# Decoder layer kernel on one core: the block that holds all five engine programs is opened without the GpSimd drain at its end

## The chip, the cores and the metric

The kernel runs on one core of one Trainium2 chip. The metric is device time in microseconds (us) of one launch. The kernel before was timed three times: 584.96, 585.82 and 586.62 us, median 585.82 us. It is written in Bass: every engine has a program of its own, and engines wait for one another by semaphores that the code names.

## The reference

One pre-norm decoder layer in float32, on x of shape (2, 1024, 256), so 2048 tokens of width 256. Cut to what is computed:

```
x = x + linear_attention(layernorm(x))      # phi(q), phi(k), k*v; two decayed prefix scans over 1024 steps
x = x + cross_attention(layernorm(x), ctx)  # 16 heads, 154 context rows, weights fside, a mask, softmax
h = layernorm(x)
y = sum over the 2 experts of 8 that each token picks: w * expert(h)    # 256 -> 352 -> 256, silu
z = shared_expert(h)
return x + y + z
```

## The kernel before, in words

`decoder(nc, A, xs, out)` (L172) allocates all buffers and semaphores, and at L378 opens one block with `nc.Block()`. In it stand five functions: the programs of TensorE (L380), ScalarE (L818), VectorE (L1071), GpSimd (L1639) and SyncE (L1791). There is no scheduler: each engine runs its program in the order in which it is written. Tokens are worked on in 16 tiles of 128, or in 4 chunks of 512. When the functions have ended, leaving the block joins the engines: this adds to each engine's program a few closing instructions, and the profile files them under L173, the line of the `with` statement whose end closes the block.

The last stage is that of the routed experts. Rows of tokens were sorted by expert into `xs_dram`; 36 slots of 128 such rows go through their expert. For each slot GpSimd issues an indirect DMA that adds the slot's 128 result rows of 256 floats to the token rows of `out_dram` (`add`, L1761; the four mixed slots take two such DMAs of 64 rows, so there are 40). Another 32 indirect DMAs of GpSimd scatter rows into `xs_dram` (L1685) earlier on. These 72 are all the DMAs that GpSimd issues; the descriptors of such a DMA are made by GpSimd itself, so each shows as a busy instruction there. All transfers that SyncE and ScalarE issue go through other queues.

Each add DMA counts up one of two semaphores, `to_out[0]` and `to_out[1]`, in turn, and a later add mostly waits for the one before it, since two slots may touch the same token. The end of the kernel is the last of these adds. SyncE's program ends with waits, so that nothing leaves the block before all of `out_dram` is written:

```
            w.wait_ge(base_out, 64)
            w.wait_ge(base_out3, 16)
            for a in (LAST[-1] - 1, LAST[-1]):
                w.wait_ge(to_out[a % 2], added(a))
```

GpSimd's own program has nothing behind its last add: it branches to the end of the block.

The closing instructions of the block use two semaphores, which stand in the program as `barrier_Pool_Activation_PE_DVE_SP_gather` and `..._release` (Pool is GpSimd, Activation ScalarE). The four other engines each raise gather by one. GpSimd waits until gather is 4, takes the 4 off again, and raises release by 4; each of the four waits for release and takes one off. The same exchange, drain of GpSimd and all, stands once at the start of the program (filed under L1997).

Of the kernel before, what the change touches and what calls it, by code (L numbers as in the profile page):

```python
# [171 lines left out]
def decoder(nc, A, xs, out):  # L172
    with ExitStack() as ctx:  # L173
# [201 lines left out]
            k, c = kc  # L375
            return bank[("pj", c, "q", 1) if k == 1 else ("q", 2 * c + 1, 7) if k == 2 else ("sm", c, 1, 2)]

        block = ctx.enter_context(nc.Block())  # L378

        @block.tensor  # L380
        def _(e):
# [1625 lines left out]
```

## Time and profile before

| what | us |
|---|---|
| median of three runs | 585.82 |
| lowest, highest | 584.96, 586.62 |
| span of the profiled execution, first to last instruction | 582.9 |
| PE (TensorE matmul) busy | 562.7 (97%) |
| DVE (VectorE) busy | 441.9 (76%) |
| ACT (ScalarE) busy | 326.0 (56%) |
| POOL (GpSimd) busy | 233.1 (40%) |

The profile is of one execution. It gives that execution's time as its span, from the first to the last instruction of the program; a device time of its own is not recorded for it. What lies around the span is what the launch adds ahead of the first and behind the last instruction, and the profile shows no instructions there; median less span is 585.82 - 582.9 = 2.9 us.

How to read the views: an engine's name with a q behind it (POOLq, SPq) is that engine's sequencer, the part that takes instructions in order, waits on semaphores and issues DMAs. Sequencer instructions are not counted as busy, so a drain never shows in the busy shares. The view of one line lists its instructions by engine and operation: how many, their durations in ns (least, median, most), and when the first and last of them began in us. EVENT_SEMAPHORE is an instruction that only waits on or changes a semaphore. DRAIN is a sequencer instruction too; its duration is the time that it stood there. DMA_INDIRECT as a busy instruction of POOL is the making of the descriptors; the transfer comes during and after it.

### The profile page before, as it was taken

What the parts mean: (1) busy time and instruction counts of PE and PEld (TensorE: products, weight loads), DVE (VectorE), ACT (ScalarE), POOL (GpSimd) and SP (SyncE); (2) the same over time, 40 slices, a digit from 0 to 9 for tenths busy, and PEclk for the clock granted to TensorE, in tenths of its full rate; (3) what the DMA queues carried; (4) which work ended last, traced back from release to release, by engine and by line L of the source; (5) the groups of instructions that cost most, each with busy time, mean ns of one, the idle gap of its engine ahead of it and who ended that gap; (6) DMA issues with size and microseconds to landing.
All of it is one profiled execution on the core that took longest, in us unless ns stands there. A gap on an engine that the chain in (4) does not pass through costs nothing.

```text
span 582.9 us, 11123 instructions
## 1 busy us (share of the span) xinstructions
PE 562.7 (97%) x3656; PEld 426.1 (73%) x3656; DVE 441.9 (76%) x838; ACT 326.0 (56%) x1005; POOL 233.1 (40%) x228
## 2 busy tenths in 40 slices
PE   8999999999999999999999999999999999999991
PEld 6547566788697978888788787878777776666661
DVE  3999999999886879958688679866677555656650
ACT  3632424368869796795976939715223245455220
POOL 1110110307580834387234671625235333353443
PEclk9999999999999999999999999999999999999997
DMA  8930004162741231423316107892645443344323
GB/s 301 347 101 2 1 1 172 45 217 91 274 155 65 100 119 45 173 74 93 127 37 218 65 20 230 270 390 87 181 111 90 67 64 58 53 70 61 54 29 35
DMA packets 36183, 68.37 MB, mean 117 GB/s; under 512 B 5504, under 2 KB 29024, under 8 KB 33632
## 3 DMA queue, kind: packets, MB, share of 16 engines
q1 hardware_dynamic: 28208, 57.99, 29.7%
q0 software_dynamic: 6784, 8.95, 9.5%
q10 hardware_dynamic: 1136, 0.73, 0.4%
q8 instruction: 30, 0.49, 0.4%
q14 instruction: 25, 0.20, 0.1%
HBM read 56.62 MB, written 15.25 MB: 123 GB/s over the span
## 4 chain that ended last, share of the span: by engine, by line
PE 58%; DVE 18%; DMA 9%; issue 7%; POOL 3%; ACT 2%; POOLq 1%; SPq 0%; DVEq 0%
PE pb L744 9%; PE pb L636 6%; DVE R L1140 6%; PE pb L499 6%; PE pb L601 6%; PE pb L549 6%; DMA out_dram<-R 5%; PE pb L565 5%; PE pb L778 5%; PE pb L516 4%; PE pb L648 3%; DVE R L1163 3%; DMA x<-in_x_dram 2%; DMA out_dram<-R,hidx 2%; PE pb L569 2%
## 5 line engine op out<-in xcount | busy, mean ns | idle before, releaser
L896 ACT ACTIVATE R<-R,mx 128x154 f32<-128x154 f32 x256 | 104.4, 415 | 0.2
L1761 POOL DMA_INDIRECT out_dram<-R x36 | 55.8, 1549 | 80.3 <-DMA out_dram<-R 33.9
L744 PE MATMUL pb<-R 128*128 x256 | 81.0, 459 | 0.0
L1022 ACT ACTIVATE R<-R 128x352 f32<-128x352 f32 x36 | 17.9, 497 | 91.6 <-DVE R L1572 80.3
L744 PEld LDWEIGHTS pb<-R 128*128 128x128 f32 x256 | 46.2, 190 | 20.4
L499 PE MATMUL pb<-xnT,wq 128*128 128x256 f32 x256 | 58.2, 383 | 0.0
L887 ACT ACTIVATE R<-pb,bq 128x256 f32<-128x256 f32 x64 | 30.1, 474 | 47.9 <-PE pb L499 47.8
L499 PEld LDWEIGHTS pb<-xnT,wq 128*128 128x128 f32 x256 | 47.7, 190 | 7.8 <-issue 1.2
L908 ACT COPY R<-pb 128x512 f32<-128x512 f32 x80 | 40.8, 614 | 18.4 <-PE pb L549 18.3
L1685 POOL DMA_INDIRECT xs_dram<-xn,pos x32 | 31.8, 993 | 47.3 <-DVE pos L1324 39.0
L896 ACT ACTIVATION_READ_ACCUMULATOR R<-R,mx 128x1 f32 x256 | 49.5, 193 | 0.0
L1660 POOL TENSOR_TENSOR sd<-mv,cst 128x4 f32<-128x4 f32 x12 | 9.8, 813 | 97.4 <-DVE mv L1088 97.3
L1219 DVE SCALAR_TENSOR_TENSOR R<-R 128x2464 f32<-128x2464 uint8 (+1 forms) x18 | 48.7, 2711 | 0.0
L778 PE MATMUL pb<-R 128*128 (+1 forms) x192 | 47.1, 381 | 1.5 <-ACT R L1031 1.5
L1208 DVE TENSOR_TENSOR R<-pb,R 128x924 f32<-128x924 f32 (+1 forms) x48 | 45.2, 998 | 2.7 <-PE pb L516 2.0
L1226 DVE TENSOR_REDUCE mx<-R 128x16 f32<-128x2464 f32 (+1 forms) x18 | 43.7, 2429 | 0.3
L636 PE MATMUL pb<-xnT,sw 128*128 128x256 f32 (+1 forms) x192 | 43.4, 381 | 0.0
L440 PE MATMUL pb<-xnT,R 128*128 128x512 f32 x96 | 43.0, 599 | 0.3 <-ACT xnT L831 0.3
L601 PE MATMUL pb<-wo,R 128*128 128x256 f32 x192 | 42.5, 380 | 0.0
L601 PEld LDWEIGHTS pb<-wo,R 128*128 128x128 f32 x192 | 36.4, 190 | 5.4 <-issue 0.4
L636 PEld LDWEIGHTS pb<-xnT,sw 128*128 128x128 f32 (+1 forms) x192 | 34.2, 181 | 7.1 <-issue 0.8
L778 PEld LDWEIGHTS pb<-R 128*128 128x128 f32 (+1 forms) x192 | 34.0, 191 | 5.7 <-issue 2.4
(202 smaller groups left out, 1180.1 us busy)
## 6 DMA issues: line engine op xcount, KB each, us to landing
R<-in_fside_dram SPq DMA_DIRECT2D x16, 1232.0 KB, 5.5
R<-in_L_ffn_w_dram SPq DMA_DIRECT2D x16, 352.0 KB
R<-in_mask_dram SPq DMA_DIRECT2D x16, 308.0 KB, 2.9
R<-xs_dram SPq DMA_DIRECT2D x32, 129.0 KB, 2.1
KV<-in_ebias_dram SPq DMA_DIRECT2D x2, 1440.0 KB
out_dram<-x SPq DMA_DIRECT2D x4, 512.0 KB, 4.7
R<-in_L_ffn_w_dram SPq DMA_DIRECT2D x8, 256.0 KB, 4.5
x<-in_x_dram SPq DMA_DIRECT2D x3, 512.0 KB, 11.4
```

Source lines behind the costliest of these rows:

```text
L440: ins = e.matmul(pb[:, u.i, :], wqkv[:, k, col * P:(col + 1) * P], xnT[:, r, k, :], start=(k == 0), stop=(k == 1))
L499: ins = e.matmul(pb[:, u.i, 0:256], wq[:, k, j * P:(j + 1) * P], xnT[:, r, k, cols], start=(k == 0), stop=(k == 1))
L601: ins = e.matmul(pb[:, u.i, 0:D], oT[:, j, q * P:(q + 1) * P], wo[:, j, :], start=(j == 0), stop=(j == 7))
L636: ins = e.matmul(pb[0:mw, u.i, q * 256:q * 256 + 256], wm[:, k, lo:lo + mw], xnT[:, r, k, cols], start=(k == 0), stop=(k == 1))
L744: ins = e.matmul(pb[:, u.i, 0:F], xsT[:, s % 2, k, :], ew13[:, bass.ds(w_reg[s] * 1408 + q * 704 + k * F, F)], start=(k == 0), stop=(k == 1))
L778: ins = e.matmul(pb[:, u.i, 0:D], sT[0:mw, s % 2, m, :], ew2[0:mw, bass.ds(w_reg[s] * 768 + m * D, D)], start=(m == 0), stop=(m == 2))
L896: ins = e.activation(att[t % 3][:, h, :], att[t % 3][:, h, :], ACT.Exp, bias=mx[:, a4, 1, h:h + 1], accum_out=mx[:, a4, 2, h:h + 1])
L908: e.copy(pT[:, hf, 2 * k:2 * k + 2, :], pb[:, u.i, :].rearrange("p (i q) -> p i q", i=2)).then_inc(free[u.i], 1)
L1208: e.tensor_tensor(att[t % 3][:, 2 * lo:2 * hi, :].rearrange("p (r h) k -> p r h k", r=2), pb[:, u.i:u.i + 2, 0:n * SK].rearrange("p r (h k ...
L1219: e.scalar_tensor_tensor(out=att[t % 3][:, lo:hi, :], in0=mk[:, s, lo:hi, :], scalar=-BIG, in1=att[t % 3][:, lo:hi, :], op0=ALU.mult, op1= ...
L1226: e.tensor_reduce(mx[:, a4, 0, lo:hi], att[t % 3][:, lo:hi, :], AX.X, ALU.max).then_inc(*topped.next((t, hs, 0)))
L1761: e.indirect_dma_start(out=out, out_offset=bass.IndirectOffsetOnAxis(ap=to.bitcast(U32), axis=0), in_=rows, in_offset=None, compute_op=ALU ...
```

## The change

One argument where the block is opened:

```diff
@@ -375,7 +375,7 @@
-        block = ctx.enter_context(nc.Block())
+        block = ctx.enter_context(nc.Block(no_gpsimd_drain=True))
 
         @block.tensor
         def _(e):
```

The five engine programs are untouched: 1105 rows of TensorE, 932 of VectorE, 406 of ScalarE, 234 of GpSimd and 286 of SyncE stand as they did, in the same order. Only the closing instructions of the block differ. In the built program they are:

```
before
  ScalarE, TensorE, VectorE, SyncE, each:
    Drain            waits release == 0, then gather + 1
    EventSemaphore   waits release >= 1, then release - 1
  GpSimd:
    Drain            (no semaphore)
    EventSemaphore   waits gather >= 4, then gather - 4
    EventSemaphore   release + 4
after
  ScalarE, TensorE, VectorE, SyncE, each:
    Drain            (no semaphore)
    EventSemaphore   waits release == 0, then gather + 1
    EventSemaphore   waits release >= 1, then release - 1
  GpSimd:
    EventSemaphore   waits gather >= 4, then gather - 4
    EventSemaphore   release + 4
```

So GpSimd's Drain is gone, and the other four have their drain and their count on gather in two instructions, where it was one. That makes 5 drains and 6 semaphore instructions before, and 4 drains and 10 semaphore instructions after. The exchange at the start of the program, with its drain, is not changed.

## Rows read from the trace of the kernel before

**Rows 1.** The page: span, busy time by engine, and the chain by engine and line.

```profile
span 582.9 us, 11123 instructions
PE 562.7 (97%) x3656; PEld 426.1 (73%) x3656; DVE 441.9 (76%) x838; ACT 326.0 (56%) x1005; POOL 233.1 (40%) x228
PE 58%; DVE 18%; DMA 9%; issue 7%; POOL 3%; ACT 2%; POOLq 1%; SPq 0%; DVEq 0%
```

**Rows 2.** The chain that ended last, its end: start us, us, what.

```profile
570.59 3.42 DMA out_dram<-R
574.01 0.88 issue
574.89 1.78 POOLq L173
```

**Rows 3.** View of line L173, the block's end.

```profile
L173 POOLq EVENT_SEMAPHORE  x2: 17/17/17, 582.7 to 582.7; - x2
L173 ACTq DRAIN  x1: 521/521/521, 569.2 to 569.2; - x1
L173 PEldq DRAIN  x1: 1320/1320/1320, 570.1 to 570.1; - x1
L173 DVEq DRAIN  x1: 524/524/524, 571.4 to 571.4; - x1
L173 POOLq DRAIN  x1: 7731/7731/7731, 574.9 to 574.9; - x1
L173 SPq COMPARE_BRANCH  x1: 41/41/41, 579.0 to 579.0; - x1
L173 SPq DRAIN  x1: 7/7/7, 579.2 to 579.2; - x1
L173 SPq EVENT_SEMAPHORE  x1: 17/17/17, 582.8 to 582.8; - x1
L173 PEldq EVENT_SEMAPHORE  x1: 51/51/51, 582.8 to 582.8; - x1
```

**Rows 4.** Timeline from 574 us: start us, us, engine, what [idle before].

```profile
572.45 1.56 POOL L1761 DMA_INDIRECT out_dram<-R  x1 [0.30 <-issue]
575.11 1.55 POOL L1761 DMA_INDIRECT out_dram<-R  x1 [1.10 <-issue]
```

**Rows 5.** Sequencer waits of SyncE from 568 us: total, times, longest.

```profile
SPq L86 <- DMA out_dram<-R: 28.0, 2, 25.3
SPq L173 <- PEq L173: 3.6, 1, 3.6
```

**Rows 6.** View of line L86, the wait helper, from 574 us.

```profile
L86 SPq EVENT_SEMAPHORE  x2: 17/22/28, 576.2 to 579.0; - x2
```

**Rows 7.** Stretches of the tail: busy by engine, PEclk, DMA share, GB/s.

```profile
576.00:578.00 2.00, 0.00 (x0) 0.00 (x0) 0.00 (x0) 0.00 (x0) 0.66 (x1) 0.50 0.40 28
578.00:580.00 2.00, 0.00 (x0) 0.00 (x0) 0.00 (x0) 0.00 (x0) 0.00 (x0) 0.50 0.25 38
580.00:582.90 2.90, 0.00 (x0) 0.00 (x0) 0.00 (x0) 0.00 (x0) 0.00 (x0) 0.50 0.00 0
```

**Rows 8.** View of line L1997, the exchange at the program's start.

```profile
L1997 DVEq DRAIN  x1: 10/10/10, 0.1 to 0.1; - x1
L1997 POOLq DRAIN  x1: 169/169/169, 0.3 to 0.3; - x1
L1997 PEldq EVENT_SEMAPHORE  x1: 51/51/51, 0.7 to 0.7; - x1
```

**Rows 9.** DMA view, issues by GpSimd: line, engine, operation, count.

```profile
out_dram<-R POOLq DMA_INDIRECT x36
xs_dram<-xn,pos POOLq DMA_INDIRECT x32
out_dram<-R,hidx POOLq DMA_INDIRECT x4
```

## The prediction

> **What bounds the kernel now.** I read the page first, then the end of the chain of waits, then the one line that the change touches, and last the stretches of the tail. The page [rows 1] says that TensorE is busy for 562.7 of 582.9 us and that the chain is 58% PE. A change that touches no matmul can still move the time, though, if it touches the part in which TensorE is no longer the bound. The chain [rows 2] shows where that is: from 570.59 us on it holds a transfer of the last adds (3.42), a wait that no record explains (0.88), and then GpSimd's sequencer in line L173 (1.78). It ends at 574.89 + 1.78 = 576.67. That is not the end of the span: the chain is followed back from the last *busy* instruction, and the last busy instruction is GpSimd's making of the descriptors of the final add, from 575.11 for 1.55 us, so to 576.66 [rows 4]. What lies behind it, 582.9 - 576.7 = 6.2 us, is in no chain and in no busy share. The reader should notice this: the chain gives GpSimd's sequencer 1% of the span, and the change acts on just the part that it leaves out.
>
> The view of the line that closes the block fills the gap [rows 3]. GpSimd's DRAIN begins at 574.9 and stands for 7731 ns, so to 574.89 + 7.73 = 582.62. Its two semaphore instructions follow at 582.7, and the other engines' last ones at 582.8; TensorE's ends at 582.8 + 0.051, and that is the end of the span. All others had been at the end of the block long before: ScalarE at 569.2, TensorE at 570.1, VectorE at 571.4, SyncE at 579.2. SyncE is the last of them since it waits for the data: its two waits on the adds ran off at 576.2 and 579.0 [rows 6], the second being the landing of the very last add. From then on it stood 3.6 us in the closing exchange [rows 5] (the row puts it down to PEq, which had been done for nine microseconds; by the rule that a wait is given to the last poster seen, the true one is GpSimd's release). The stretches agree [rows 7]: in 576 to 578 and 578 to 580 us the DMA engines are still at 0.40 and 0.25; in 580 to 582.9 they are at 0.00, and so is everything else. For 2.9 us and more the chip does nothing that the kernel needs: the drain alone holds the end.
>
> **The change part by part.**
>
> GpSimd's DRAIN goes. Before, the end is set by the later of two arrivals, the drain's end at 582.62 and SyncE's count at 579.2. Without the drain GpSimd is at its wait on gather from 574.9 on, and what is late next is SyncE, and thus the landing of the last add. That landing does not move by this edit, as the add is issued before the block's end on the same engine in both kernels.
>
> The exchange itself stays. From the end of the drain to the end of the span it took 582.85 - 582.62 = 0.23 us. The same exchange at the start of the program [rows 8] gives a second price: from the drain's end at 0.3 + 0.17 = 0.5 to TensorE's end at 0.7 + 0.05 = 0.75 it took some 0.25 us (rounded rows, so 0.2 to 0.3). I take 0.23.
>
> Four drains and four counts become separate instructions. Three engines have 7 us and more to spare. On SyncE the count now comes one instruction later than its DRAIN of 7 ns: a semaphore instruction of SyncE costs 17 to 28 ns [rows 3, 6], and the nearest gap between two of its instructions is that from the branch (579.0 + 0.04) to the drain (579.2), some 0.1 to 0.2. So between 0.02 and 0.2 us; I take 0.05, near to the instruction's own duration, since no branch lies between. It can't be below nothing: an instruction is added in front of the count.
>
> The sum: SyncE's drain at 579.2, plus 0.05 for its own count, plus 0.23 for the exchange, gives an end at 579.5 us. Span before 582.9, so the change takes away 582.9 - 579.5 = 3.4 us (bounds 3.2 with the slow end of both terms, 3.5 with the fast end). The launch's surroundings of 2.9 us I leave as they are. The profiled execution with its 582.9 + 2.9 stands for the median here, as the 2.9 is the median less the span. So 585.8 - 3.4 = **582.4 us**, 0.58% less. About 0.3%, or 1.8 us, is what a measurement of this kernel can tell from no change (its three runs lie within 1.66 us), so a gain of 3.4 is visible.
>
> What the drain waits for is the one open quantity, and it matters for the rivals. It outlasts the landing of the last transfer at 579.0 by 582.62 - 579.0 = 3.6 us, so it is not just a wait for the data. The drain at the start of the program, with no DMA of GpSimd behind it, took 169 ns [rows 8]. At the end 36 + 32 + 4 = 72 of them lie behind it [rows 9]. From the end of the last descriptor-making, 576.66, to the drain's end are 5.96 us, which would be 0.083 us for each of the 72. Either reading (3.6 us after the landing, or 5.96 of work from 576.66 on) fits this one trace; both drop out of the span when the DRAIN does.
>
> **Rivals.**
>
> *The drain is only put off.* Behind the program the launch has an ending of its own, part of the 2.9 us around the span. If that ending needs GpSimd to be idle in the same sense, then what was paid in the block is paid there: GpSimd would be ready at 582.62 as before, whoever asks. The span in the profile would shrink by 3.4 and the time would not, 585.8 us. For it: 2.9 us is room for instructions on all engines, and the program's own start has such a drain. Against it: the trace shows none behind the span, and data has landed at 579.0, so nothing needs waiting for. The start's drain of 169 ns [rows 8] and the 3.6 us left over here weigh about alike, and I give it one chance in five.
>
> The Trainium skill bears on this: "VectorE: DVE Perf Modes", section "The DRAIN you can't avoid", tells of drains that the runtime adds ahead of and behind a program on all five engines, about 12 ns each. No row here shows those behind the span. If there is one on GpSimd, it stands at 12 ns only because the block's drain came before it, and without that it would be the one that takes the 3.6 us; by this rule the time stays at 585.8. "Runtime: NRT & Kernel Launch", section "The ~15µs preamble/postamble breakdown", adds that resetting semaphores and re-arming DMA rings ends every launch; by that the ending has a reset of its own, which need not wait. By that second page the time would follow the span.
>
> *The drain is put off and starts over; slower.* This is the second reading of the open quantity: the 5.96 us are work of GpSimd that starts when it is asked for (0.083 us for each of the 72 DMAs). Before, 579.2 - 576.66 = 2.5 us of it lay beside the last transfer. If the launch's ending asks for it, it starts only at 579.5, runs alone, and ends at 579.5 + 5.96 = 585.5, where it was 582.62 (plus the exchange, 582.85): 2.6 us later, 588.4 us. It decides against me if both hold, that the ending asks and that the work is by the count of DMAs. For it: 3.6 us after the last landing is hard to explain by waiting. Against: what was against the first rival.
>
> *It doesn't do what it says.* The argument acts on the closing instructions alone; the drain at the start is left (169 ns, hidden behind nothing, no change). GpSimd's drain is gone in the built program, so I give this no chance of its own. A variant is that the last add's landing comes later or earlier by chance: adds take 3.4 us of transfer each in the chain [rows 2], and a few tenths of scatter go into the range.
>
> **How the numbers follow.** Forecast, 3.4 us less at 582.4: 0.72. Put off at equal price, 585.8: 0.19. Put off and started over, 588.4: 0.07. The rest, 0.02, is a gain that comes out under 0.3%, split between the ending and the span. The likeliest case has its own range: the sum's bounds are 582.3 to 582.6, and the scatter of medians (runs 0.9 below and 0.8 above theirs) widens it to 581.5 to 583.3. That holds nearly all of its 0.72. To leave out no more than 2 in 10 it has to reach into the first rival, to 586.0, which takes in a half of it and more. Range 581.4 to 586.0. Chances: faster by over 0.3% (below 584.1) 0.72; within 0.3% 0.20; slower by over 0.3% (above 587.6) 0.08.
>
> **What the profile of the changed kernel would show.** The view of L173 has no POOLq DRAIN; it has two semaphore instructions each on ACTq, PEldq, DVEq and SPq, and two on POOLq, the first of which begins within 0.1 us of SyncE's count. SyncE's wait in the closing exchange falls from 3.6 to about 0.2 us. The span is 579.5 us, give or take 0.3, and the stretch behind the last landing is 0.5 us long. Everything up to 575 us stands at the same times within 0.2. If the span is 579.5 and the time stays near 585.8, the drain was put off; if the time is near 588.4, it was put off and starts over. The forecast is wrong altogether if the span itself stays near 582.9, for then something else than the drain held GpSimd.

## The result: 0.54% faster, by the drain that left the end

| | median us | lowest, highest | runs |
|---|---|---|---|
| kernel before | 586.14 | 584.96, 587.65 | 6 |
| changed kernel | 582.54 | 581.2, 583.38 | 6 |

The ratio is 0.9946, 95% interval 0.9932 to 0.996: 3.2 us less, 2.3 to 4.0 (the two medians of the table lie 3.6 us apart, within that interval). Timed again beside other kernels (five runs of it, 15 of before) it was 0.9956, 0.9943 to 0.997, so 2.6 us, 1.8 to 3.3. The forecast was 582.4 us, 3.4 us less.

For the six runs of the changed kernel, and for all runs of the experiments below, the span of each run is recorded too. Kept apart: the kernel before has a median span of 583.95 us (28 runs, beside e1 to e4) and 583.3 (15 runs, beside e5 to e8), the changed one of 580.6 (6 runs) and 580.7 (5). What lies around the span, the time less the span, was 1.81 to 1.82 us in the median for the kernel before, and 1.92 to 1.94 for the changed one.

### The profile page after: what moved, and what is told of

Its sections match the earlier page's. It is cut to its first block, busy times and chain, and to the rows that moved or that the text cites. A ratio compares the mean times of both kernels' runs of the same rounds, so it can differ in the third digit from the quotient of the medians.

```text
span 581.5 us, 11126 instructions
## 1 busy us (share of the span) xinstructions
PE 562.7 (97%) x3656; PEld 426.0 (73%) x3656; DVE 441.7 (76%) x838; ACT 326.0 (56%) x1005; POOL 232.7 (40%) x228
## 4 chain that ended last, share of the span: by engine, by line
PE 56%; DVE 20%; DMA 9%; issue 8%; POOL 4%; ACT 2%; POOLq 0%; DVEq 0%; SPq 0%
PE pb L744 7%; DMA out_dram<-R 6%; PE pb L636 6%; DVE R L1140 6%; PE pb L499 6%; PE pb L601 6%; PE pb L549 6%; PE pb L565 5%; PE pb L516 4%; PE pb L648 4%; PE pb L778 4%; DVE R L1163 3%; PE pb L613 2%; PE pb L569 2%; DMA out_dram<-R,hidx 2%
```

## The profile after

The profiled execution of the changed kernel took 583.38 us with a span of 581.5. The busy times on the page are those of before but for tenths, as in [rows 1]; there are three instructions more, 11126.

```profile
span 581.5 us, 11126 instructions
PE 562.7 (97%) x3656; PEld 426.0 (73%) x3656; DVE 441.7 (76%) x838; ACT 326.0 (56%) x1005; POOL 232.7 (40%) x228
```

The view of L173, which answers to [rows 3]; the columns are count, durations in ns, and when the first and last began:

```profile
L173 PEldq EVENT_SEMAPHORE  x2: 51/51/51, 571.4 to 581.4; - x2
L173 SPq EVENT_SEMAPHORE  x2: 17/17/17, 581.2 to 581.4; - x2
L173 POOLq EVENT_SEMAPHORE  x2: 17/17/17, 581.3 to 581.3; - x2
...
L173 SPq COMPARE_BRANCH  x1: 41/41/41, 581.0 to 581.0; - x1
L173 SPq DRAIN  x1: 7/7/7, 581.2 to 581.2; - x1
```

There is no POOLq DRAIN. SyncE's drain begins at 581.2, its count on gather follows at 581.2, GpSimd answers at 581.3, and TensorE's last semaphore instruction ends at 581.45. SyncE's waits, as in [rows 5]:

```profile
SPq L86 <- DMA out_dram<-R: 28.5, 2, 25.7
SPq L173 <- PEq L173: 0.2, 1, 0.2
```

Where SyncE stood 3.6 us in the closing exchange, it stands 0.2. The order of the ends has turned round: the landing of the last add, which ends SyncE's second wait at 580.9, now sets the end.

```profile
L86 SPq EVENT_SEMAPHORE  x2: 17/22/28, 578.1 to 580.9; - x2
```

The end of the chain, against [rows 2]:

```profile
572.50 3.42 DMA out_dram<-R
575.92 1.11 issue
577.03 1.55 POOL out_dram L1761
```

The GpSimd sequencer in L173 is gone from it. The chain again stops at the last descriptor-making (577.03 + 1.55 = 578.58), so the landing and the exchange, 2.9 us, stand in it no more than the drain did. But the reader should see another thing: the last descriptor-making begins at 577.03, where it was 575.11 in [rows 4]. The whole tail stands 1.9 us later than in the profile of before. The span of this pair of profiles therefore fell by 1.4 us only, while the times fell by 3.2. The experiments say which of the two to believe.

## The experiments

Three readings of the drain were open: it ends a fixed time after the last landing; it is work of a fixed price from the moment at which GpSimd is free; or it is work by the count of DMAs. And one rival on the time: that it is only put off. "Engine free" below is the end of the last descriptor-making, 576.66 us in the profile of before.

**The drain put back by hand.** `e1_own_drain` is the changed kernel with this at the end of GpSimd's program:

```diff
                 if s < 4:
                     scatter_rows(3, 1, s)
+            e.drain()
```

> The block is opened without the GpSimd drain, as in the changed kernel, and GpSimd's own program ends with one explicit drain. If the drain alone was what cost 3.6 us, it comes back whole: a POOLq DRAIN of about 7.7 us, ending 3.7 us after the last landing, and the time of the kernel before (ratio 1.00). If the gain came from the other form of the closing exchange (counts in instructions of their own), the time stays near that of the changed kernel (0.994).

Measured: ratio to before 1.0009, 0.9991 to 1.0027. The explicit drain:

```profile
L1790 POOLq DRAIN  x1: 7731/7731/7731, 576.0 to 576.0; - x1
```

7731 ns, the same to the nanosecond as in [rows 3], though this execution reached it 1.2 us later. So the instruction alone is the cost, not the form of the exchange. One small thing does go with the form: the time less the span is 1.92 us here as in the changed kernel, against 1.82 in those that keep the old closing exchange. The changed form gives back 0.1 us outside the span; why is open.

**The drain asked for after the landing.** `e2_land_then_drain`, on the kernel before:

```diff
                 if s < 4:
                     scatter_rows(3, 1, s)
+            for a in (LAST[-1] - 1, LAST[-1]):
+                w.wait_ge(to_out[a % 2], added(a))
```

> The kernel before, but GpSimd waits for the last two adds to land ahead of the block's drain. Theory landing (the drain ends a fixed 3.6 us after the last landing, whenever it was asked for): DRAIN lasts 3.6 us, time as before (ratio 1.00). Theory work (5.96 us of work from the moment it is asked for with GpSimd free): DRAIN lasts 6.0 us from the landing, the span ends 2.3 us later, ratio 1.004. Theory plain wait (the drain only waits for data): DRAIN under 0.3 us, ratio 0.994.

Measured: ratio 1.0056, 1.004 to 1.0071.

```profile
L173 POOLq DRAIN  x1: 5948/5948/5948, 579.0 to 579.0; - x1
```

All data had landed, and the drain still took 5.95 us, as it does from the engine's being free in the kernel before (574.89 + 7.73 - 576.66 = 5.96). The reading "fixed time after the landing" falls: the drain is work that starts when asked for. This also prices the overlap that the kernel before had, some 2.3 us beside the last transfer (the span of this execution is 2.3 us longer; the times say 3.3 us, 2.3 to 4.2).

**A second drain early, and two in a row.** `e3_mid_drain` and `e4_two_drains`, both on the kernel before. The first added drain is that of e3 alone, the second that of e4 alone:

```diff
             add_sb2(3)
+            e.drain()                      # e3
             w.wait_ge(placed.sem, placed[3])
...
                     scatter_rows(3, 1, s)
+            e.drain()                      # e4
```

> The kernel before with one more drain in GpSimd's program, behind 24 of its 72 DMAs, where it waits for VectorE anyway (ahead of the scatter of the last chunk). Theory count (0.083 us for each GpSimd DMA not yet drained): the middle drain lasts 24 x 0.083 = 2.0 us though all its data landed long ago, and the last one has 48 DMAs to do: it ends at 576.66 + 4.0 = 580.6 us where it was 582.6, ratio 0.997. Theory landing: the middle drain lasts 0.2 us or less, the last one ends 3.6 us after the landing as before, ratio 1.00. Theory work with a fixed price: the middle drain lasts 6.0 us, the last one as before, ratio 1.00.

> The kernel before with an explicit drain of GpSimd straight ahead of the block's own, so two in a row at the end. Theories count and landing: the first takes 7.7 us as the single one did, the second finds nothing to do and lasts 0.2 us or less, ratio 1.00. Theory fixed price: the second costs 3.6 to 6.0 us more, ratio 1.006 to 1.010.

Measured: e3 0.9969 (0.9948 to 0.9991), e4 1.0002 (0.9983 to 1.0021). In e3 the early drain stood for 9663 ns from 397.3, most of it behind work that GpSimd had queued; its last instruction ahead of the drain ended at 404.87, so 2.05 us were its own. The last drain of e3, and the two of e4:

```profile
L173 POOLq DRAIN  x1: 6056/6056/6056, 575.0 to 575.0; - x1
```

```profile
L1790 POOLq DRAIN  x1: 7731/7731/7731, 576.7 to 576.7; - x1
...
L173 POOLq DRAIN  x1: 47/47/47, 584.5 to 584.5; - x1
```

24 DMAs, 2.05 us; 48 DMAs, 575.0 + 6.06 less the engine's being free at 576.77, 4.28 us (count says 4.0; the 0.3 us over it are not explained); 72 DMAs, 5.96; none, 0.05. So the price is by the DMAs that GpSimd has issued since its last drain, long landed or not. The fixed price falls with e4. A drain put where GpSimd waits anyway takes its share off the end: e3 is 1.8 us faster than before (0.5 to 3.0) by doing more.

**More DMAs.** Three kernels issue 48 more DMAs in the idle stretches of GpSimd before 100 us, each 8 bytes of 16 rows (`e5_48_small`) or of 128 rows (`e6_48_large`; `e7_48_large_no_drain` is the same on the changed kernel), and `e11_40_large` 40 of 128 rows. The edit, in e6:

```diff
+        spare = sb("spare", (P, 48, 2))
+        extra = sem("extra")
...
-            for kc in NORMS[0:6]:
+            for n, kc in enumerate(NORMS[0:6]):
                 rooting(*kc)
+                if n in (2, 3, 4):
+                    for i in range(16):
+                        e.dma_start(spare[0:128, 16 * (n - 2) + i, :], A["cst"][0:128, 0:2]).then_inc(extra, 16)
+            e.wait_ge(extra, 16 * 48)
             add_bo(0)
```

> The kernel before with 48 more DMAs issued by GpSimd between 35 and 100 us, where it is idle; each moves 16 rows of 8 bytes into a spare tile that nobody reads. Theory count of DMAs (0.07 to 0.083 us each, whatever their size): the last drain ends 3.4 to 4.0 us later against the end of the last descriptor-making (9.4 to 9.9 us behind it where it was 5.95), ratio 1.006 to 1.007. Theory count of rows (the cost goes by the descriptors, 128 or 64 rows for each of the 72): 48 x 16 rows are 8% more than 72 x 128, the drain takes 0.4 to 0.5 us more, ratio 1.001. A rival, that only indirect DMAs cost: nothing is added, ratio 1.00.

> As the run with 48 more small DMAs, but each of the 48 moves 128 rows of 8 bytes. Theory count of DMAs: the same drain as with 16 rows, 9.4 to 9.9 us behind the last descriptor-making. Theory count of rows: 48 x 128 rows are 67% more, so again 9.4 to 9.9 us, but only 6.4 us with 16 rows. Ratio 1.006 to 1.007 for both theories; the pair of runs tells them apart.

> The changed kernel (no GpSimd drain at the block's end) with the same 48 more DMAs of 128 rows. If the drain is only put off into the launch's ending, the time less the span grows from 1.9 us by what 120 DMAs cost there (3 us and more). If it is gone, the time less the span stays 1.9 us and the time is that of the changed kernel, ratio 0.994 to 0.995 against the kernel before, though the same kernel with the drain is at 1.006.

Measured: e5 1.0068 (1.0053 to 1.0084), e6 1.0014 (1.0001 to 1.0027), e7 0.9947 (0.9932 to 0.9962). The last drains of e5 and, below it, e6:

```profile
L173 POOLq DRAIN  x1: 11652/11652/11652, 577.6 to 577.6; - x1
```

```profile
L173 POOLq DRAIN  x1: 7733/7733/7733, 576.1 to 576.1; - x1
```

e5 is as the count has it: 3.92 us more for 48, 0.0817 us each. e6 is what neither theory allowed: 48 larger DMAs added 2 ns. The chain of e6 shows one trace of the 48. Between the wait that ends with a landing and the making of the third last add's descriptors, GpSimd stands 0.61 us longer than in the kernel before; here that piece, first before, then in e6:

```profile
569.88 0.49 issue
```

```profile
570.55 1.10 issue
```

This pause comes after 117 of the 120 DMAs, and e7 has it at the same place. It is about what e6 is slower by (0.8 us, 0.1 to 1.6).

e7 does its own task all the same. With 120 DMAs issued, of which a drain would have counted 72 by e6, and no drain, the time less the span is 1.90 us and the time that of the changed kernel, so nothing of the drain is paid in the launch's ending. That ends both rivals in which it is put off. Nor does the exchange at the start of a program show it: GpSimd's drain there is as short in the changed kernel as in [rows 8], and as in e1, which drains at its end.

```profile
L1997 POOLq DRAIN  x1: 171/171/171, 0.3 to 0.3; - x1
```

**What a drain costs, measured by itself.** To see why e6 paid nothing, two kernels on the changed one put groups of such DMAs early, wait for them to land, and drain. Each ran once, and only its drains are read. The edit in `e9_drain_ladder`, with `spare` and `extra` as in e6:

```diff
-            for kc in NORMS[0:6]:
+            issued = 0
+            groups = {0: ((4, 16),), 1: ((16, 16),), 2: ((16, 128),), 3: ((32, 128),), 4: ((16, 64),)}
+            for n, kc in enumerate(NORMS[0:6]):
                 rooting(*kc)
+                for many, few in groups.get(n, ()):
+                    for i in range(many):
+                        e.dma_start(spare[0:few, i, :], A["cst"][0:few, 0:2]).then_inc(extra, 16)
+                    issued += many
+                if n in groups:
+                    e.wait_ge(extra, 16 * issued)
+                    e.drain()
```

> The changed kernel, with five groups of extra DMAs in the stretches before 110 us where GpSimd is idle, each group waited for until it has landed and then followed by an explicit drain: 4 of 16 rows, 16 of 16 rows, 16 of 128 rows, 32 of 128 rows, 16 of 64 rows. As all data has landed, each drain shows the bookkeeping alone. Theory count, with old entries given up when room is needed (so that the run with 48 DMAs of 128 rows had lost them by the end): drains of 0.3, 1.3, 1.3, 2.6 and 1.3 us, by 0.082 us each, whatever the rows. Theory size (a DMA of 128 rows of 8 bytes leaves no entry, one of 16 does): 0.3, 1.3, under 0.2, under 0.2 and, for 64 rows, one or the other. The time of the whole says nothing, since the groups delay GpSimd.

The five drains of e9, each from the view of its line in a stretch of its own:

```profile
L1729 POOLq DRAIN  x1: 387/387/387, 15.6 to 15.6; - x1
...
L1729 POOLq DRAIN  x1: 1344/1344/1344, 33.9 to 33.9; - x1
...
L1729 POOLq DRAIN  x1: 1350/1350/1350, 47.6 to 47.6; - x1
...
L1729 POOLq DRAIN  x1: 2651/2651/2651, 82.2 to 82.2; - x1
...
L1729 POOLq DRAIN  x1: 1344/1344/1344, 98.3 to 98.3; - x1
```

4, 16, 16, 32 and 16 DMAs: 0.06 us and (2651 - 387) / 28 = 81 ns for each, whether of 16, 64 or 128 rows. The count holds, and the size does not matter to the drain. `e10_long_ladder` has the groups 48, 72, 96 and 120 of 128 rows and 120 of 16, with a wait for landing after each 48:

> The changed kernel with five groups of extra DMAs early in GpSimd's program, each waited for and then drained: 48, 72, 96 and 120 of 128 rows, and 120 of 16 rows. With nothing given up the drains take 0.06 + 0.0816 us for each: 4.0, 5.9, 7.9, 9.9 and 9.9 us. If old entries are given up once their rows fill the room there is, the drains of the large ones stop growing with a group somewhere between 72 and 120 (the run with 48 large ones ahead of the 72 of the kernel showed only 72), or fall back, while 120 of 16 rows still take 9.9 us. The time of the whole says nothing, as the groups delay GpSimd by hundreds of us in all.

```profile
L1731 POOLq DRAIN  x1: 3986/3986/3986, 44.2 to 44.2; - x1
...
L1731 POOLq DRAIN  x1: 5922/5922/5922, 92.0 to 92.0; - x1
...
L1731 POOLq DRAIN  x1: 7877/7877/7877, 158.4 to 158.4; - x1
...
L1731 POOLq DRAIN  x1: 609/609/609, 241.8 to 241.8; - x1
...
L1731 POOLq DRAIN  x1: 9837/9837/9837, 306.3 to 306.3; - x1
```

72 are 5.92 us, which is the kernel's own drain. The fourth fell to 0.61 us, the price of 7. The timeline of GpSimd there says what happened:

```profile
224.95 8.94 POOL L1727 DMA_DIRECT2D spare<-in_cst_dram  x17 [1.62 <-DMA spare<-in_cst_dram]
236.78 3.69 POOL L1727 DMA_DIRECT2D spare<-in_cst_dram  x7 [2.90 <-issue]
```

After 48 + 48 + 17 = 113 DMAs of 128 rows GpSimd stopped for 2.90 us with no releaser, then issued the last 7, and only those 7 were left for the drain. 120 DMAs of 16 rows made it stop nowhere. One reading is that GpSimd keeps an entry for each DMA until a drain, that the entries take room by rows, and that old ones are given up when the room is full. e6 fits its place: of the 117 DMAs ahead of the pause eight are of 64 rows, so they have the rows of 113 large ones. `e11_40_large` stays under that room:

> The kernel before with 40 more DMAs of 128 rows of 8 bytes early on, where the run with 48 of them showed no longer drain and a stall without a named cause ahead of its third last add. In the long ladder the same stall stood behind 113 DMAs of 128 rows, and the drain then found 7. Theory room: entries are kept until a fixed room is full (113 DMAs of 128 rows, the 64-row ones taking about half), then old ones are given up. 40 + 72 DMAs, eight of them of 64 rows, stay under it: no stall ahead of the third last add, and a drain of 112 entries, 0.06 + 112 x 0.0816 = 9.2 us from the end of the last descriptor-making (5.95 before), ratio 1.0055, so slower than with 48. Theory size (extra DMAs of 128 rows far ahead of the end cost nothing for another reason): 5.95 us, ratio 1.001.

```profile
L173 POOLq DRAIN  x1: 9367/9367/9367, 575.3 to 575.3; - x1
```

Measured: ratio 1.003, 1.0012 to 1.0048. The engine was free at 577.06, so the drain's own part is 575.29 + 9.37 - 577.06 = 7.59 us, 1.64 more than before. At 0.082 each that is 20 of the 40, not 40 and not none. Both theories miss. The theory of room misses twice, for it also allowed no pause, and e11 has one: not ahead of the third last add, but earlier, after 95 DMAs. The same piece of the chain there, first before, then in e11:

```profile
519.47 0.48 issue
```

```profile
519.21 1.04 issue
```

So e6, e10 and e11, whose drains cost less than the count of all DMAs, each have a pause, and e5, whose drain costs the full count of 120, has none like it. But the pauses come at the rows of 113, 113 and 94 large DMAs since the last drain. One fixed room does not give all three. What sets off a pause, and how many entries go with it, stays open; whether it goes by all that was issued since the start of the program and not since the last drain was not tested.

**The changed kernel again**, to see its spans and the tail:

> The changed kernel once more, beside the others on one chip. Ratio 0.994 to 0.995 if the gain is 2.5 to 3.5 us; time less span 1.9 us; spans scattered over 2 us with the landing of the last add (579 to 581.5), while TensorE ends at 571.3 to 571.8 in each profile.

Measured: 0.9956, as told above; time less span 1.92; spans 579.3 to 581.0. GpSimd's last add, first of this execution, then of e4, which keeps the drain:

```profile
576.39 1.55 POOL L1761 DMA_INDIRECT out_dram<-R  x1 [1.10 <-issue]
```

```profile
576.92 1.55 POOL L1761 DMA_INDIRECT out_dram<-R  x1 [1.20 <-issue]
```

The last add begins at 575.11 (before), 575.16 (e2), 575.22 (e3), 576.27 (e1), 576.39 (e8), 576.92 (e4) and 577.03 (after). Kernels with the drain lie from 575.11 to 576.92, and of those without it e7 is earliest of all, at 574.45. So the 1.9 us between the two first profiles is scatter of the add chain and no effect of the change.

## Why the prediction was right

*Where the end is set.* Right. That the part behind the last busy instruction belonged to the drain is shown by e1, which brings back the 7731 ns and the time with one instruction.

*The sum.* Its terms hold. The step from SyncE's drain to the end was put at 0.05 + 0.23 us and took 581.45 - 581.17 = 0.28. For an equal landing the span falls by 582.85 - (579.22 + 0.28) = 3.35 us, forecast 3.4. Outside the span 0.1 comes back. The two comparisons gave 3.2 and 2.6, and their intervals hold 3.25. That the median of 582.54 lies 0.1 us from the forecast is in part luck: the kernel before stood at 586.14 beside it, not at 585.82.

*The landing does not move.* Right as to the change, wrong for the pair of profiles: it moved by 1.9 us by chance. I had put "a few tenths" for this; the profiles of this kernel and its variants scatter over 1.9 us, and over 2.6 with e7. So two of the signs named ahead failed: the span of the profile was 581.5 us, not 579.5 give or take 0.3, and the times up to 575 us were not those of before within 0.2. The others held: no drain, 0.2 us of waiting, 0.5 us behind the last landing. A reader who had judged by the spans of the two profiles alone would have found 1.4 us and named the wrong step.

*The surroundings.* I took 2.9 us as median less span; they are 1.8. The profile of before was of a short execution, its span 0.4 to 1.1 us under the medians of its kernel. The difference of 1.1 us hid in this term and cancelled, since it stood on both sides of the subtraction.

*What the drain does.* I left two readings open. e2 decides for work from the moment of asking, e3, e5, e9 and e10 for the count, at 0.082 us each, close to the 0.083 worked out ahead. The rival that was slower had the right mechanism for the drain, and failed on the other half of its condition: the launch's ending does not ask for it (e7).

*The rivals that it is put off.* Both fall with the time less the span: 1.92 to 1.94 us in the changed kernel and 1.90 with 48 more DMAs. The Trainium skill, "VectorE: DVE Perf Modes", section "The DRAIN you can't avoid", tells of drains that the runtime adds on all five engines; if GpSimd has one in the ending, it does not do this work. The trace shows none, so that is as far as the runs go.

## What to carry to other kernels

Look at what stands between the last busy instruction and the end of the span: the chain of waits doesn't cover it, and here 6.2 us lay there, of which 3.4 could go. A kernel that issues many DMAs from GpSimd and whose last waits already prove that all has landed pays for a drain that proves nothing more; leave it out, or, where one is needed, put another one earlier where GpSimd waits anyway. Judge a change of 3 us by the timed medians and by terms measured against the same landmark in each trace, not by the spans of two single profiles.

## What the runs showed of the hardware that was not expected

A drain of GpSimd cost 0.06 us and 0.082 us for each DMA that GpSimd had issued since its last drain, landed or not: 0.39 us for 4, 5.92 for 72, 9.84 for 120 of 16 rows, and 1.34 to 1.35 for 16 DMAs whether of 16, 64 or 128 rows. Three kernels with many DMAs of 128 rows paid less at the drain, and each had a pause of GpSimd ahead of it: 2.90 us after 113 such DMAs since the last drain, with a drain of 0.61 us, the price of 7 (e10); 0.61 us after 117 of 120, with a drain that cost 72 (e6); 0.56 us after 95 of 112, with a drain that cost 92 (e11). That old entries are given up in the pause is inferred from these numbers, and the rule behind it was not found.
